# A mixture-of-experts loop on one NeuronCore: the operand of a tile turned three tiles ahead, the inner result two tiles back, the down product four tiles back

## What is computed

```python
topv, topi = jax.lax.top_k(logits, TOP_K)
rw = jax.nn.softmax(topv.astype(jnp.float32), axis=-1).astype(x.dtype)
W = jnp.zeros((N, E), x.dtype).at[jnp.arange(N)[:, None], topi].set(rw)
gu = jnp.einsum('nh,eih->nei', x, gu_w)
gate, up = (gu[..., :I], gu[..., I:])
inter = jax.nn.silu(gate) * up
inter_w = inter * W[:, :, None]
out = jnp.einsum('nei,ehi->nh', inter_w, dp_w)
```

## Time and profile before

| | us |
|---|---|
| median of three timed runs | 969.02 |
| the profiled execution: its span, the only time the profile gives of it | 1061.7 |
| of it: up to the expert loop | 394.0 |
| of it: expert loop, 160 tiles | 589.5 |
| of it: sums and stores after the loop | 78.2 |
| TensorE busy over the span | 944.7 (89%) |
| VectorE, ScalarE, GpSimd busy over the span | 547.2, 263.6, 479.2 |

### The profile page before, as it was taken

One profiled execution on the slowest core, in us unless ns is written; L12 is line 12 of the kernel. 1 busy time (PEld: TensorE's weight loads), 2 busy tenths in 40 slices (PEclk: granted clock), 3 DMA queues, 4 the chain that ended last, 5 costly groups with the idle time before them and its releaser, 6 DMA issues.

```text
span 1061.7 us, 18602 instructions
## 1 busy us (share of the span) xinstructions
PE 944.7 (89%) x3569; PEld 571.9 (54%) x3570; DVE 547.2 (52%) x1460; ACT 263.6 (25%) x789; POOL 479.2 (45%) x468
## 2 busy tenths in 40 slices
PE   7999999999995688989998889989898999887697
PEld 2434544544534246766766666667575666665243
DVE  4676776687685443433433334343434334343888
ACT  2122222222212103323323323233332233232000
POOL 0000066045266664555565555556565655555500
PEclk9999999999996898999999999999999999999699
DMA  9922021003021424666566666666567665797697
GB/s 345 330 69 75 1 67 28 40 1 95 0 62 43 136 80 148 222 201 216 199 193 208 241 225 212 229 199 227 197 222 227 207 213 196 250 403 263 230 420 312
DMA packets 68518, 192.06 MB, mean 181 GB/s; under 512 B 19926, under 2 KB 20438, under 8 KB 68104
## 3 DMA queue, kind: packets, MB, share of 16 engines
q1 hardware_dynamic: 38232, 120.28, 32.6%
q0 software_dynamic: 30256, 71.43, 20.5%
HBM read 158.98 MB, written 52.54 MB: 199 GB/s over the span
## 4 chain that ended last, share of the span: by engine, by line
PE 66%; another core or an unknown queue 8%; issue 7%; DVE 5%; DMA 4%; DVEq 1%; ACT 1%; ACTq 1%; POOLq 0%; POOL 0%; SPq 0%
PE bank L1661 19%; PE bank L1669 11%; PE bank L1434 7%; PE bank L1656 6%; PE bank L1479 5%; PE bank L1730 4%; PE bank L1445 4%; PE bank L1543 3%; PE bank L1676 2%; DMA front<-y_rows 2%; PE bank L1562 2%; DMA front<-h_rows,gid 1%; DVE front L1297 1%; PE bank L1456 1%
## 5 line engine op out<-in xcount | busy, mean ns | idle before, releaser
L1661 PE MATMUL bank<-wqkv,h2T 128*128 x1280 | 310.7, 387 | 0.0
L631 POOL DMA_INDIRECT y_rows<-front,sid x160 | 164.7, 1030 | 202.7 <-issue 90.7
L1661 PEld LDWEIGHTS bank<-wqkv,h2T 128*128 128x128 f32 x1280 | 236.6, 195 | 26.7
L583 POOL DMA_INDIRECT slot_table<-pair,place x128 | 131.1, 1024 | 249.6 <-DVE place L1025 186.5
L621 POOL DMA_INDIRECT front<-h_rows,gid x167 | 172.1, 1030 | 68.5 <-issue 46.0
L1311 DVE COPY front<-bank 128x128 f32<-128x128 f32 x160 | 46.6, 291 | 268.4 <-remote 154.4
L1669 PE MATMUL bank<-wqkv,front 128*128 x320 | 171.3, 618 | 1.3 <-DVE front L1311 1.3
L817 ACT ACTIVATE h2T<-bank 128x512 f32<-128x512 f32 x162 | 96.5, 596 | 245.8 <-PE bank L1656 145.4
L1656 PEld LDWEIGHTS bank<-const,front 128*128 128x128 f32 x648 | 82.1, 144 | 100.4 <-issue 97.2
L1305 DVE COPY front<-bank 128x512 f32<-128x512 f32 x160 | 110.0, 688 | 40.7 <-PE bank L1669 28.8
L1434 PE MATMUL bank<-wqkv,front 128*128 128x512 f32 x256 | 117.3, 610 | 8.3 <-DVEq L957 6.2
(11 more groups left out here) (247 smaller groups left out, 775.2 us busy)
## 6 DMA issues: line engine op xcount, KB each, us to landing
wqkv<-in_experts SPq DMA_DIRECT2D x64, 768.0 KB
front<-y_rows SPq DMA_DIRECT2D x20, 768.0 KB, 9.3
wqkv<-y_rows SPq DMA_DIRECT2D x12, 768.0 KB, 11.7
front<-in_w_mod SPq DMA_DIRECT2D x5, 1024.0 KB, 10.5
x<-in_x SPq DMA_DIRECT2D x4, 1024.0 KB, 11.2
h_rows<-h SPq DMA_DIRECT2D x4, 1024.0 KB
out_dram<-x SPq DMA_DIRECT2D x16, 256.0 KB, 7.8
wqkv<-in_w_in SPq DMA_DIRECT2D x3, 1024.0 KB, 13.6
```

Source lines behind the costliest of these rows:

```text
L583: pool.indirect_dma_start(out=slots[:, :], out_offset=bass.IndirectOffsetOnAxis(ap=place[b % 2][:, i, k:k + 1], axis=0), in_=pair[:, b * T ...
L631: pool.indirect_dma_start(out=y_rows[:, :], out_offset=bass.IndirectOffsetOnAxis(ap=sid[:, s:s + 1], axis=0), in_=yb[s % YBUFS], in_offset ...
L1661: mm = pe.matmul(bank[2 + s % 2][:, 0:GU], xT[s % 4][:, k, :], wqkv[:, bass.ds(w + k * GU, GU)], start=(k == 0), stop=(k == KC - 1))
```

## The change

TensorE's slot becomes: turn x of tile t+3, gate and up of t, turn inner of t-2, down of t-4. `take_x` runs one tile further ahead on ScalarE; on VectorE `take_inter` is of t-2 and `take_y` of t-4; GpSimd's step s scatters tile 8r+s-2 in place of 8r+s, and still gathers 8r+s+8. The buffers `act`, `inter` and `iT` become rings of four. Gate, up and the turned inner of one tile now share one bank of a ring of four (2, 3, 6, 7); so `gate_up` of t waits until inner of t-4 was copied out. The banks of x (0, 1) and of down (4, 5), the four places of the turned x, the eight of the gathered x and the four `yb` stay as they are.

```diff
+RING = 4
+TURN_AHEAD = 3
+FIRST_TURNS = [(2,), (3,), (4,), (5,), (6,), (7, 8), (9,), (10,)]
+INTER_BACK = 2
+STORE_BACK = 2
+DOWN_BACK = 4
...
-        act, inter, iT = ([region[5][:, (2 * j + i) * P:(2 * j + i + 1) * P] for i in range(2)] for j in range(3))
+        act = [region[3][:, 3 * D + i * P:3 * D + (i + 1) * P] for i in range(RING)]
+        inter, iT = ([region[5][:, (RING * j + i) * P:(RING * j + i + 1) * P] for i in range(RING)] for j in range(2))
...
+        tile_bank = [bank[i] for i in (2, 3, 6, 7)]
+        gu_bank = [b[:, 0:GU] for b in tile_bank]
+        inter_bank = [b[:, GU:GU + P] for b in tile_bank]
...
-                    put_rows(r * ROUND + s, s)
+                    if not isinstance(r, int) or s >= STORE_BACK:
+                        put_rows(r * ROUND + s - STORE_BACK, (s - STORE_BACK) % ROUND)
...
-                    take_x(r * ROUND + s + 2, s + 2)
+                    for n in FIRST_TURNS[s] if isinstance(r, int) else [s + TURN_AHEAD]:
+                        take_x(r * ROUND + n, n)
...
-                    if not (isinstance(t, int) and t < 1):
-                        take_inter(t - 1, (s - 1) % 2)
+                    if not (isinstance(t, int) and t < INTER_BACK):
+                        take_inter(t - INTER_BACK, (s - INTER_BACK) % ROUND)
                     gated(t, s)
-                    if not (isinstance(t, int) and t < 2):
-                        take_y(t - 2, r if s >= 2 else r - 1, (s - 2) % ROUND)
+                    if not (isinstance(t, int) and t < DOWN_BACK):
+                        take_y(t - DOWN_BACK, r if s >= DOWN_BACK else r - 1, (s - DOWN_BACK) % ROUND)
...
             def gate_up(t, s, w):
+                if not (isinstance(t, int) and t < RING):
+                    pe.wait_ge(s_iT, t - RING + 1)
...
-                    turn(t + 2, r + (s + 2) // ROUND, (s + 2) % ROUND)
+                    for n in [s + TURN_AHEAD] if again else FIRST_TURNS[s]:
+                        turn(r * ROUND + n, r + n // ROUND, n % ROUND)
...
-                    if again or t >= 1:
-                        turn_inter(t - 1, (s - 1) % 2)
-                    if again or t >= 2:
-                        down(t - 2, (s - 2) % 2, w[s - 2])
+                    if again or t >= INTER_BACK:
+                        turn_inter(t - INTER_BACK, (s - INTER_BACK) % ROUND)
...
+                    if again or t >= DOWN_BACK:
+                        down(t - DOWN_BACK, (s - DOWN_BACK) % ROUND, w[s - DOWN_BACK])
```

More of the change, by code:

```diff
@@ L666, in _ @@
                     round_pool(r)
+            for n in range(STORE_BACK):
+                put_rows(used * ROUND - STORE_BACK + n, ROUND - STORE_BACK + n)
             for n in range(AHEAD):
@@ L1294, in gated @@
                 ve.wait_ge(s_sl, t + 1)
[L1295 to L1298, removed]
+                if not (isinstance(t, int) and t < RING):
+                    ve.wait_ge(s_I, t - RING + 1)
+                ve.scalar_tensor_tensor(out=inter[s % RING], in0=gu_bank[s % RING][:, INNER:GU],
+                                        scalar=wgt[:, s:s + 1], in1=act[s % RING],
                                         op0=ALU.mult, op1=ALU.mult).then_inc(s_in, 1)
@@ L1308, in take_inter @@
                 ve.wait_ge(s_I, t + 1)
-                if not (isinstance(t, int) and t < 2):
-                    ve.wait_ge(s_d, t - 1)
-                ve.tensor_copy(iT[s % 2], bank[6 + s % 2][:, 0:P]).then_inc(s_iT, 1)
+                if not (isinstance(t, int) and t < RING):
+                    ve.wait_ge(s_d, t - RING + 1)
+                ve.tensor_copy(iT[s % RING], inter_bank[s % RING]).then_inc(s_iT, 1)
             LISTS = [(), (5,), (6,), (7, 8), (9, 10), (11, 12), (13,), (14,)]
@@ L1342, in _ @@
                     round_ve(r)
-            take_inter(used * ROUND - 1, ROUND - 1)
-            take_y(used * ROUND - 2, used - 1, ROUND - 2)
-            take_y(used * ROUND - 1, used - 1, ROUND - 1)
+            for n in range(DOWN_BACK):
+                if n < INTER_BACK:
+                    take_inter(used * ROUND - INTER_BACK + n, ROUND - INTER_BACK + n)
+                take_y(used * ROUND - DOWN_BACK + n, used - 1, ROUND - DOWN_BACK + n)
             tf = Tally(s_fm)
@@ L1659, in gate_up @@
             def gate_up(t, s, w):
+                if not (isinstance(t, int) and t < RING):
+                    pe.wait_ge(s_iT, t - RING + 1)
                 for k in range(KC):
-                    mm = pe.matmul(bank[2 + s % 2][:, 0:GU], xT[s % 4][:, k, :], wqkv[:, bass.ds(w + k * GU, GU)],
+                    mm = pe.matmul(gu_bank[s % RING], xT[s % 4][:, k, :], wqkv[:, bass.ds(w + k * GU, GU)],
                                    start=(k == 0), stop=(k == KC - 1))
@@ L1673, in turn_inter @@
                 pe.wait_ge(s_in, t + 1)
[L1674 to L1678, removed]
+                pe.transpose(inter_bank[s % RING], inter[s % RING], ident).then_inc(s_I, 1)
+            kept = [pe.alloc_register(f"pe_at_{DOWN_BACK - n}_back") for n in range(DOWN_BACK + 1)]
+            kept_loads = pe.alloc_register("pe_next_loads")
             def expert_of(t):
@@ L1723, in _ @@
             end = used * ROUND
-            turn_inter(end - 1, 1)
-            for n in range(2):
-                down(end - 2 + n, n, pe.snap(kept[n], min_val=0, max_val=(WSLOTS - 1) * WROW))
+            for n in range(DOWN_BACK):
+                if n < INTER_BACK:
+                    turn_inter(end - INTER_BACK + n, ROUND - INTER_BACK + n)
+                down(end - DOWN_BACK + n, ROUND - DOWN_BACK + n, pe.snap(kept[n], min_val=0, max_val=(WSLOTS - 1) * WROW))
             def late_row(g, k):
@@ L1730, in late_row @@
                 return pe.matmul(sum_bank[g % BACK][:, :], ident, back[g % BACK][k], start=(k == BY_PE - 1), stop=(k == BY_PE - 2))
-            pe.wait_ge(s_xT, end + 2)
+            pe.wait_ge(s_xT, end + TURN_AHEAD)
             apart(pe)
```

23 lines of the change are left out of this document (12 added, 11 removed).

## The result

The change is slower: 1016.91 us, the median of 4 runs, against 969.64 us for the kernel before. The ratio is 1.046, with a 95% interval of 1.0438 to 1.0482. That is 47 us more, where the prediction had 15 more and 1000 us as its upper end.

A forecast was written before the change was run, and what follows sets the result against it. TensorE was taken to bound the expert loop, at 3.13 us per clean slot. Work, VectorE waits, gathered x and last rounds gave 0.9 - 4 + 13.6 + 5 = +15.5 us on 969.0: 984 us, 8-in-10 range 958 to 1000.

The forecast's parts named there:

- the gathered x: Turning of each round's last tile: arrival 4.0 us against 3.24 lead, 13.6 us in 17 rounds plus 5 in the last two.
- Work: TensorE's instructions per tile unchanged; one more turning and a longer tail after the last gate and up: +0.9 us.
- The waits for VectorE and ScalarE: TensorE's waits before turning inner: deeper rings cover late hand-overs, -4 us, bounds 0 and 18 regained.
- the 88 us over the floor: Profiled expert loop, 589.5 us, against 160 tiles at 3.13 us, 501; 15 us assumed left in the timed runs.
- The lead of 3.24 us: Time from GpSimd's gather of tile 8r+7 to its turning one slot earlier; the longest in 19 rounds.
- The last two rounds: Waits for x at the loop's end, where results are read back: 2.5 us each, 5 in all.
- The weights: Loads of expert weights wait for downs two slots, 6.3 us, later: taken as 0, other end 5 us at the loop's end.
- the case in which x always takes 5.2 us: Every gather arrives after 5.2 us, all 42 us of waits: 1012 us if nothing is regained, 1000 with 12 regained.
- the first: Rival: late hand-overs are in the timed runs and two slots absorb them; faster, 952 to 962 us, chance 0.22.
- the second: Rival: x arrives within 3.24 us unprofiled and late hand-overs are the profiler's; no difference, 970 us, chance 0.13.
- The third: Rival: later downs uncover weight loads at the loop's end, +5 us on top of some x waits; 990 us, chance 0.12.
- The signs that the prediction named: Profile after: tile 8r+7 waits for its gather in most rounds, gap before turning inner under 15 us, clean slot 3.13.

The follow-up runs named there:

- e9: The kernel before with GpSimd's scatter one step behind, so gathers are issued one slot earlier: 973.76 us, ratio 1.0015.
- e10: The change's rings of four for banks and small buffers, with all distances as in the kernel before: 971.55 us, ratio 0.9998.
- e12: The kernel before with each load of weights asked for two downs later, nothing else moved: 976.78 us, ratio 1.0038.
- e6: e1 with only the first eighth of each expert's weights loaded from expert 5 on: 973.99 us, ratio 1.002.
- e1: The change with x turned two tiles ahead instead of three: 983.68 us, ratio 1.0116.
- e8: The kernel before, unedited, profiled a second time: span 971.7 us, time 973.63 us.
- e2: The change with GpSimd's scatter three steps behind instead of two: 986.3 us, ratio 1.0144.
- e7: The change with the down of t-3 instead of t-4: 982.8 us, ratio 1.0104.
- e11: The kernel before with x turned three tiles ahead and the scatter one step behind: 977.39 us, ratio 1.0062.
- e5: The kernel before with x turned three ahead and only an eighth of each expert's weights loaded from expert 5 on: 997.5 us, ratio 1.0264.

## Why the prediction was wrong in size

The sign and the mechanism were right, and the step that failed is the size of the term "the gathered x": an arrival of 4.0 us and 13.6 + 5 us in all, where the profile has arrivals of 4.9 to 5.7 us in nine of 17 rounds and 29.0 + 8.9 us. A second step failed with it, the 4 us that the prediction took off for VectorE's waits. Against the second profile, in the order of the prediction's steps:

- *Work*: I had 0.9 us. The stretch behind the last gate and up is 2.3 us longer (84.7 against 82.4). Too small by more than half. The other profiles with the down of t-4 have 84.6 to 85.9 us there, those with the down of t-2 81.1 to 83.2, but 87.7 in e9; so the place of the down is not shown to be the whole cause.
- *The waits for VectorE and ScalarE*: I had -4. It is 0: TensorE stands idle 0.8 us there in the second profile, and the rings alone (e10) change nothing that can be told. I had assumed that 15 of the 88 us over the floor are in the timed runs, and 9 of them in this wait; the loop of the second profile is 7.7 us over, and none of them is a wait for VectorE before the turning of inner. The lead of 3.24 us is right, the lateness of everything else in that execution was not. A rule of the Trainium skill ("Perfetto Trace Analysis", section "Optimization Strategy") was weighed for this side, of recurring gaps as a sign of too few buffers. It did not hold here: the gaps were not in the second profile, whose span fits the timed runs, so no buffer could take them away.
- *The gathered x*, 17 rounds: I had 0.8 us each, 13.6 in all. Measured by the starts of gate and up from tile 6 to 143, the slots are 29.9 us over, against 0.9 before: 29.0, or 1.7 a round. Of the 29.9, 23.2 lie in the slots that turn the last tile of a round, 1.7 in the slot after tile 111's, at the lower clock (below), and 5 elsewhere, most of it in waits for other tiles, the longest 1.46 us in front of tile 18: the prediction had nothing for those. I took an arrival of 4.0 us, the middle between 2.9 and 5.2. There are two arrivals and little between them, 3.5 to 4.0 and 4.9 to 5.7, and the upper holds in 9 of 17 rounds. The trace of before had a second sign of this that I did not use: the turning of tile 79 waited too, and started 5.33 us after its gather. Both waits in the body that the trace puts down to a last tile's gather were over 5 us, and I averaged them with a bound from round 0. Such a wait also costs more than its own length. In the round of tile 39 the slot takes 5.27 us, 2.13 more than 3.14, for a wait of 1.92, since the turning can no longer overlap the end of the down. After the wait of 2.40 us in front of tile 111 the granted clock falls from the upper of TensorE's two levels (2.4 GHz) and is for most of 4 us at the lower one (1.2):

```profile
749.00:751.40 2.40, 0.03 (x1) 0.04 (x1) 0.85 (x2) 0.00 (x0) 1.19 (x2) 1.00 1.00 382
751.40:755.40 4.00, 4.00 (x13) 3.18 (x14) 0.00 (x0) 0.90 (x3) 2.24 (x3) 0.57 0.59 180
755.40:758.00 2.60, 2.60 (x14) 1.93 (x13) 1.43 (x4) 1.01 (x4) 0.00 (x0) 1.00 0.21 78
```

  (Stretches of the change, columns as above: 0.57 of the full clock in the mean of 4 us, and the gate and up in it takes 3.58 us instead of 1.89.)
- *The last two rounds*: I had 5 us. From tile 143 on the excess is 10.7 us against 1.8: 8.9, near the 8 of my upper bound.
- *Round 0* (up to tile 6): I had nothing for it. It is 7.4 us over against 5.0, so 2.4. This differs between profiles even of kernels that turn x two tiles ahead, from 3.6 (e12) to 7.2 (e6, whose loop starts early).
- *The weights*: I took 0 and 5 as the other end. In the change it is 0, since TensorE already waits for x. With x in time it is 9.7 us by the medians (e1 against e6) and nearly 7 by the slots of their profiles, both above my bound: I had counted the slots of the downs, and not that SyncE's reads wait for the scatters ahead of the last loads.

29.0 + 8.9 + 2.4 + 2.3 = 42.6 us is the difference of the two spans, 1014.3 - 971.7, and of the two times, 1016.25 - 973.63. The medians differ by 47.3: the profiled execution of before (e8) took 4.0 us more than the median of 969.64, and that of the change 0.7 less than its own. Against the 972.2 to 972.5 of the experiments the loss would be 44 to 45 us.

My upper end of 1000 held the case in which x always takes 5.2 us only together with 12 us regained. Without them that case was worked out in the prediction as 1012, and left out. Of the rivals, the first (late hand-overs in the timed runs) fell with e8 and e10, the second with every profile after it. The third is real in e1, e2 and e7, but not what made this change slow. The signs that the prediction named came: tile 8r+7 waits for its gather in 19 of 20 rounds, the gap in front of L1691 is 0.1 us, and a slot that waits for nothing takes 3.14 us. The span that it expected for the profiled execution, 1030 to 1090 us, did not: it is 1014.3.

The gap between a profile's own time and the timed run can be weighed once more. The time is above the span of the same execution by 1.8 to 2.1 us in every profile but the first, whose own time is not on record. The Trainium skill ("Runtime: NRT & Kernel Launch", section on the 15 us of preamble and postamble) gives a gap of about 6.2 us that is the same for all kernels, with the profile's total as the larger of the two. These rows agree that the gap is small and steady, and differ in size and sign; the span from the first to the last instruction is what they measure, which may not be the total that the page means. I read the 92.7 us as evidence against that rule; they were evidence against the profiled execution.

## What to carry to other kernels

When one step of a software pipeline is moved earlier, find what issues its input, and what paces that issuer: here GpSimd's gather stood behind a scatter that had not moved, and moving both (e11, e2) took most of the loss away. A transfer's arrival has no single value when another transfer shares the engines: sort its arrivals by what was issued beside them before one is picked, and check whether the larger load falls beside it in the same phase again and again. A profiled execution whose span is 10% over the timed runs is good for orders and distances, not for its waits.

## What was not expected of the hardware

A load of 768 KB issued 0.72 us after a gather of 128 rows delays the gather's arrival from 3.4 to 3.9 us (with 96 KB, e5) to between 4.9 and 5.7 us, in every such round of the change from tile 15 to 143; one issued 2.4 us or more ahead leaves it at 3.5 to 4.0 in the change. Not every trace is as clean: in the second profile of before, tile 119, with its load 2.4 us ahead, takes 5.3 us. How the two transfers hold each other up, no run here tells.

The profiled execution shown before the prediction has its hand-overs from TensorE up to 3.4 us late and many semaphore records missing, while the second profile of the same kernel shows nearly every slot at 3.14 us. What disturbs such an execution stays open; no run here tells it.
